# A fused adaLN block of attention and mixture of experts: the experts' rows gated by gathered gate rows before their scatter, and half of the late second rows loaded without accumulation

## The reference

```
mod = (silu(c) @ wmod).reshape(4, 6, 1, 256)
sa, ca, ga, sb, cb, gb = mod rows; ga, gb kept at least 0.25 from zero
h = layernorm(x) * (1 + ca) + sa
x = x + ga * attention(h)               # one head of 128, softmax over 2048 keys
h = layernorm(x) * (1 + cb) + sb
shared = (silu(h @ shared_gate.T) * (h @ shared_up.T)) @ shared_down.T       # I = 512
probs = sigmoid(h @ router_w.T + bias)  # 8 experts
scores, indices = top_k(probs, 2); scores = scores / sum(scores)
combined = sum over the two experts of score * expert(h)                     # I = 512
x = x + gb * (shared + combined)
```

## Time and profile before

| | us |
|---|---|
| median of three runs | 1621.56 |
| the three runs | 1619.24, 1621.56, 1622.91 |
| the profiled execution, its own time | 1623.41 |
| its span on the core | 1621.8 |

### The profile page before, as it was taken

The page is one execution under the profiler, slowest core; times in us unless marked ns, Lnnn a source line. Parts: engine busy times, 40 slices in busy tenths (PEclk is TensorE's granted clock), DMA queues, the critical chain, the costliest instruction groups (busy, mean ns, idle before and its releaser), DMA issues.

```text
span 1621.8 us, 37347 instructions
## 1 busy us (share of the span) xinstructions
PE 1585.6 (98%) x12578; PEld 1525.2 (94%) x12579; DVE 1204.2 (74%) x2492; ACT 994.4 (61%) x1735; POOL 528.8 (33%) x597
## 2 busy tenths in 40 slices
PE   8999999999999999999989999999999999999998
PEld 6799999999999998999989999999999999999987
DVE  6678787777778777898776676766666666666687
ACT  5566666666665556666655666666666666666653
POOL 2545445232300001477761222222222222222321
PEclk9999999999999999999999999999999999999999
DMA  3233343111101326322243132133133231111796
GB/s 124 85 117 125 118 143 124 53 46 45 35 27 37 134 111 186 109 96 92 95 149 95 57 104 65 58 110 110 58 98 94 88 107 62 55 61 41 185 268 184
DMA packets 69610, 160.36 MB, mean 99 GB/s; under 512 B 12932, under 2 KB 17924, under 8 KB 68872
## 3 DMA queue, kind: packets, MB, share of 16 engines
q1 hardware_dynamic: 44872, 93.96, 17.4%
q0 software_dynamic: 23248, 62.97, 13.2%
q10 hardware_dynamic: 1392, 2.10, 0.4%
HBM read 90.75 MB, written 68.24 MB: 98 GB/s over the span
## 4 chain that ended last, share of the span: by engine, by line
PE 48%; DVE 6%; DMA 3%; issue 1%; POOL 1%; ACT 1%; POOLq 0%; DVEq 0%; ACTq 0%; SPq 0%
PE f_bank L957 30%; PE f_bank L32 5%; PE f_bank L34 5%; PE f_bank L33 5%; PE f_bank L939 2%; DMA w_all<-y_rows 2%; POOL x_rows L1420 1%; DVE f_prod L1012 1%; DVE f_aT_lo L1004 1%; DMA y_rows<-more_rows,goes_to 1%; DVE xT_lo L1085 1%; PE f_bank L930 1%; DVE more_rows L1053 0%; DVE more_rows L1059 0%; DVE Z L1763 0%
## 5 line engine op out<-in xcount | busy, mean ns | idle before, releaser
L957 PE MATMUL f_bank<-xT_hi,w_cur_hi 128*128 128x256 f32 x1136 | 322.0, 283 | 0.7 <-ACT f_silu_g L992 0.7
L957 PE MATMUL f_bank<-xT_hi,w_cur_lo 128*128 128x256 f32 x1136 | 321.9, 283 | 0.0
L957 PE MATMUL f_bank<-xT_lo,w_cur_hi 128*128 128x256 f32 x1136 | 321.9, 283 | 0.0
L1438 POOL DMA_INDIRECT y_rows<-more_rows,goes_to x142 | 139.0, 979 | 436.1 <-ACT more_rows L1536 250.2
L1917 DVE TENSOR_TENSOR w_cur_lo<-w_all,w_cur_hi 128x1024 fp32r<-128x1024 f32 x142 | 173.5, 1222 | 63.4 <-ACT w_cur_hi L1503 63.4
L1012 DVE TENSOR_TENSOR f_prod<-f_silu_g,f_bank 128x512 f32<-128x512 f32 x206 | 141.6, 687 | 104.2 <-PE f_bank L957 102.5
L957 PEld LDWEIGHTS f_bank<-xT_hi,w_cur_hi 128*128 128x128 f32 x1136 | 218.0, 192 | 0.8 <-issue 0.8
L957 PEld LDWEIGHTS f_bank<-xT_hi,w_cur_lo 128*128 128x128 f32 x1136 | 218.4, 192 | 0.0
L957 PEld LDWEIGHTS f_bank<-xT_lo,w_cur_hi 128*128 128x128 f32 x1136 | 218.2, 192 | 0.0
L957 PE MATMUL f_bank<-xT_hi,w_shared 128*128 128x256 f32 x1024 | 204.1, 287 | 3.8 <-DVE xT_lo L1744 3.3
L418 ACT ACTIVATE prob<-s_pair,negmax 128x1024 f32<-128x1024 f32 x128 | 142.0, 1114 | 90.4 <-DVE negmax L770 90.4
(11 more groups left out here) (295 smaller groups left out, 4392.7 us busy)
## 6 DMA issues: line engine op xcount, KB each, us to landing
more_rows<-x_rows POOLq DMA_DIRECT2D x71, 260.0 KB, 3.0
XS<-in_x SPq DMA_DIRECT2D x32, 256.0 KB, 3.2
XR<-in_x SPq DMA_DIRECT2D x32, 256.0 KB, 2.9
x<-XR SPq DMA_DIRECT2D x32, 256.0 KB, 2.1
Z<-x SPq DMA_DIRECT2D x4, 2048.0 KB, 11.6
w_all<-y_rows SPq DMA_DIRECT2D x32, 256.0 KB, 5.8
w_all<-y_rows POOLq DMA_DIRECT2D x32, 256.0 KB, 7.0
out<-Z SPq DMA_DIRECT2D x31, 256.0 KB, 4.9
```

The source lines that it names most:

```text
L957: mm = pe.matmul(out[:, 2 * P * i:2 * P * i + 2 * P], w, x, start=(c == 0 and n == 0), stop=(c == HC - 1 and n == 2))
L1438: pool.indirect_dma_start(d.y_rows, bass.IndirectOffsetOnAxis(ap=goes_to[:, par, t:t + 1], axis=0), y[:, t, :], None).then_inc(y_sent[t], 16)
```

## The change

1. **Experts' outputs are gated before they are scattered.** SP writes the four gate rows to a new small DRAM tensor `gates` (4 x 256). For each pair, DVE works out each row's batch from `goes_to` (one more small instruction in `tell`, so `told` counts five per pair), POOL fetches each row's gate with an indirect DMA into `gate_rows` (`fetch_gates`, two per pair), and DVE multiplies the two output tiles at once (`gate_outputs`, 128 x 512, in the next step, ahead of that step's second product). The scatter waits for this multiply (`y_gated`) instead of ACT's copy.
2. **The shared gate goes into the weights.** `shared_down` is now split four times, once for each batch, multiplied by that batch's gate row on POOL: 14 pieces instead of 11. The down weights of the second to fourth batch are loaded when their tiles come near (`load_down`; batches 1 and 3 into a new tile `w_down`, batch 2 over batch 0). `gated` goes; `shared_out` adds PSUM to `Z` directly, early and late; `add_late` and `gate_chunk` go.
3. **Late chunks.** Chunks are taken in order. For slots 0, 2, 4 and 6 of eight (`BESIDE`) SP loads the second row plainly beside the first, and DVE adds both with two instructions; for the others POOL's accumulating DMA stays and DVE adds once. The scattered rows are laid out by batch, so `tokens` and `y_v` change. The last product of DVE moves behind the chunks, ahead of the tail.
4. **The plan of the pairs** is spread over steps 34 to 38 instead of 34 to 37, and the first split of weights comes a step later.
5. **Prologue.** SP loads two chunks of x, then waits for the modulation's columns before the third. ACT waits for wqkv and writes its high part before it issues the loads of the mask, wo and the modulation's rows.
6. ACT writes the first two normalised rows somewhat earlier at the end of the attention, and in the last pair one `single_high` ahead of the outputs.

```diff
-            for m in range(NG + 4):
+            chunk(0)
+            chunk(1)
+            sp.wait_ge(cols_loaded, 16)
+            for m in range(2, NG + 4):
                 chunk(m)
...
             def split_piece(i):
-                pool.wait_ge(piece_in, 16 * i + 16)
+                pool.wait_ge(piece_in, loads_up_to(i))
+                if of_gated(i):
+                    by_chunk = piece_raw[:].rearrange("p (c h) -> p c h", h=H)
+                    pool.tensor_tensor(by_chunk, by_chunk, gate_row[:].unsqueeze(1).to_broadcast([P, W // H, H]),
+                                       ALU.mult).then_inc(piece_split, 1)
+                    pool.wait_ge(piece_split, splits_up_to(i) - 2)
                 pool.tensor_copy(piece_hi[:], piece_raw[:]).then_inc(piece_split, 1)
-                pool.wait_ge(piece_split, 2 * i + 1)
+                pool.wait_ge(piece_split, splits_up_to(i) - 1)
                 pool.tensor_tensor(piece_raw[:].bitcast(F32R), piece_raw[:], piece_hi[:].bitcast(F32),
                                    ALU.subtract).then_inc(piece_split, 1)
...
             act.dma_start(w_raw, wqkv).then_inc(w_loaded, 16)
             act.wait_ge(c_loaded, 16)
             act.activation(ce[:], cT[:], ACT.Exp, scale=-1.0).then_inc(silu_c, 1)
+            act.wait_ge(w_loaded, 16)
+            act.activation(w_hi[:], w_raw, ACT.Copy).then_inc(w_split, 1)
+            act.dma_start(wo_raw, wo).then_inc(wo_loaded, 16)
+            act.dma_start(mask_i[:], mask).then_inc(wo_loaded, 16)
             for n in range(2):
                 o = 2 * H + 512 * n
                 act.dma_start(wmod_rows[:, n], wm[:, :, o:o + 512]).then_inc(rows_loaded, 16)
-            act.dma_start(wo_raw, wo).then_inc(wo_loaded, 16)
-            act.dma_start(mask_i[:], mask).then_inc(wo_loaded, 16)
-            act.wait_ge(w_loaded, 16)
-            act.activation(w_hi[:], w_raw, ACT.Copy).then_inc(w_split, 1)
...
-            sp.wait_ge(gy_done, ALL)
-            sp.wait_ge(sent[0], ONCE * (GROUPS // RING))
+            sp.wait_ge(f.y_out, ALL)
+            for i in range(2):
+                sp.wait_ge(sent[i], ONCE * (GROUPS // RING))
             sp.wait_ge(d.w_ready, 64)
...
             def load(k):
-                n = C * chunk_order[k]
-                sp.dma_start(slots[:, k % SLOTS], y_v[0, :, n:n + C, :]).then_inc(y_in[k % SLOTS], 16)
-
+                n = C * k
+                sp.dma_start(slots[:, k % SLOTS], y_v[0, n // TB, :, n % TB:n % TB + C, :]).then_inc(y_in[k % SLOTS], 16)
+                if k % SLOTS in BESIDE:
+                    sp.dma_start(second[:, k % SLOTS], y_v[1, n // TB, :, n % TB:n % TB + C, :]
+                                 ).then_inc(y_sum[k % SLOTS], 16)
...
-            def scatter(j, par):
-                for t in range(2):
-                    if t == 1 or inside(j - 1, NP):
-                        hold(pool, d, y_sent[1 - t], 16 * j + 16 * t)
-                    hold(pool, d, y_copied, 2 * j + t + 1)
-                    pool.indirect_dma_start(d.y_rows, bass.IndirectOffsetOnAxis(ap=goes_to[:, par, t:t + 1], axis=0),
-                                            y[:, t, :], None).then_inc(y_sent[t], 16)
+            def scatter(j, par, t):
+                if t == 1 or inside(j - 1, NP):
+                    hold(pool, d, y_sent[1 - t], 16 * j + 16 * t)
+                hold(pool, d, y_gated, j + 1)
+                pool.indirect_dma_start(d.y_rows, bass.IndirectOffsetOnAxis(ap=goes_to[:, par, t:t + 1], axis=0),
+                                        y[:, t, :], None).then_inc(y_sent[t], 16)
+
+            def fetch_gates(j, par, t):
+                hold(pool, d, told, 5 * j + 5)
+                if inside(j - 1, NP):
+                    hold(pool, d, y_gated, j)
+                pool.indirect_dma_start(gate_rows[:, t, :], None, d.gates,
+                                        bass.IndirectOffsetOnAxis(ap=batch[:, par, t:t + 1], axis=0)
+                                        ).then_inc(gate_in[t], 16)
...
+                for t in range(2):
+                    if inside(j - 1, NP):
+                        scatter(j - 1, 1 - par, t)
+                    fetch_gates(j, par, t)
...
-            def gated(m):
+            chunks_added = []
+
+            def shared_out(m):
                 dve.wait_ge(f.y_mm, m + 1)
-                if m == 0:
-                    dve.wait_ge(gate_loaded, 80)
-                dve.tensor_tensor(gys[m >= L0][:, m % 2, :], f.y_bank[m % 2][:, 0:H], rows[:, tile_of(m) // TB, 0:H],
-                                  ALU.mult).then_inc(f.y_out, 1)
-
-            def shared_out(m):
-                dve.wait_ge(f.y_out, shared_count(m))
+                k = tile_of(m) // C
+                if k in chunks_added:
+                    dve.wait_ge(out_done, k + 1)
                 z = Z[:, d.home(tile_of(m)), :]
-                dve.tensor_tensor(z, gys[m >= L0][:, m % 2, :], z, ALU.add).then_inc(gy_done, 1)
+                dve.tensor_tensor(z, f.y_bank[m % 2][:, 0:H], z, ALU.add).then_inc(f.y_out, 1)
```

On DVE, in the pair step and in the late stage:

```diff
                 dve.tensor_tensor(score[:, par, :], score[:, par, :], ride[:, par, :, 2], ALU.add).then_inc(told, 1)
+                dve.tensor_scalar(batch[:, par, :], goes_to[:, par, :], (P * TB).bit_length() - 1, NB - 1,
+                                  ALU.logical_shift_right, ALU.bitwise_and).then_inc(told, 1)
+
+            def gate_outputs(j):
+                dve.wait_ge(y_copied, 2 * j + 2)
+                for t in range(2):
+                    hold(dve, d, gate_in[t], 16 * j + 16)
+                dve.tensor_tensor(y, y, gate_rows, ALU.mult).then_inc(y_gated, 1)
...
+            def output_chunk(k, tiles_added):
+                n = C * k
+                own = Z[:, d.home(n):d.home(n) + C, :]
+                dve.wait_ge(f.y_out, min(tiles_added, n + C))
                 dve.wait_ge(y_sum[k % SLOTS], 16 * (k // SLOTS + 1))
-                c = chunk_order[k]
-                if ALL + FIRST <= C * c < NT - C:
-                    dve.wait_ge(f.y_out, shared_count(L0 + C * c + C - 1 - ALL))
-                gate = rows[:, C * c // TB, 0:H].unsqueeze(1).to_broadcast([P, C, H])
-                dve.tensor_tensor(slots[:, k % SLOTS], slots[:, k % SLOTS], gate, ALU.mult).then_inc(gated_done, 1)
-
-            def output_chunk(k):
-                n = C * chunk_order[k]
-                own = Z[:, d.home(n):d.home(n) + C, :]
-                dve.wait_ge(gy_done, min(ALL + FIRST, max(ALL, n + C)))
-                dve.wait_ge(gated_done, k + 1)
+                if k % SLOTS in BESIDE:
+                    dve.wait_ge(y_in[k % SLOTS], 16 * (k // SLOTS + 1))
+                    dve.tensor_tensor(own, own, second[:, k % SLOTS], ALU.add).then_inc(second_added, 1)
+                    dve.wait_ge(second_added, len([c for c in range(k + 1) if c % SLOTS in BESIDE]))
                 dve.tensor_tensor(own, own, slots[:, k % SLOTS], ALU.add).then_inc(out_done, 1)
...
@@ -1978,11 +2041,12 @@
                     plan_counts()
                 if n == STEPS + 3:
                     plan_ends()
+                if n == STEPS + 4:
                     plan_starts()
-                if n == STEPS + 4:
                     plan_behind()
+                if n == STEPS + 5:
                     plan_experts()
-                if n == STEPS + 5:
+                if n == STEPS + 6:
                     plan_moves()
                     plan_rows()
...
+                else:
+                    gate_outputs(j - 1)
                 f.dve_products(dve, m1, f.up_home(k1))
 
             pairs(dve, step)
             for i in range(LATE):
                 m = L0 + i
-                if 3 <= i < 3 + FIRST:
-                    gated(m - 3)
+                if i == 2:
+                    gate_outputs(NP - 1)
+                if i >= 3:
...
-                f.dve_products(dve, m, f.up_home(m))
+                if i < LATE - 1:
+                    f.dve_products(dve, m, f.up_home(m))
                 for k in chunks_of[i]:
-                    gate_chunk(k)
-                    output_chunk(k)
+                    output_chunk(k, ALL + max(0, i - 2))
```

170 lines of the change are left out of this document (96 added, 74 removed).

## The result

The changed kernel took 1668.82 us in the median of three runs (1667.47 to 1672.28) where the kernel before took 1621.56: a ratio of 1.0293, 95% interval 1.0278 to 1.0308. It is slower by 47 us. The prediction was 1620, with a range up to 1636.

What follows compares the result with a forecast made beforehand. PE was taken to bound the kernel nearly everywhere. Terms -0.7 - 2.8 - 0.35 + 1.7 + 9 - 4.4 - 3.7 = -1.25 took the profiled 1623.4 us to 1622.2, the median 1621.56 to 1620; range 1612 to 1636.

Steps and rivals of the forecast that it cites:

- the landing g: Experts' stage: time for gather 1 to land, put at 2.4 to 3.0 us and taken as 2.75.
- What bounds the kernel, prologue: PE sets the time nearly everywhere, only its 36 us idle can be won; delaying the third x chunk gives -0.7 us.
- The ring: Experts' stage: multiply, scatter 0, scatter 1, gather 1, next multiply; 6.23 + g, taken as 8.98 us, within the 9.06 period.
- rival 1: Experts' stage: the ring sets the period once g is over 2.83; 1630 us at g = 2.9, 1637 at 3.0; chance 0.28.
- What doesn't fit is a transfer that lands late.: Experts' stage: late scatters reach PE with 6 us, gather 1 adds half as much; loss +9 us, bounds +3 and +16.
- DVE itself: Experts' stage: multiply, small instruction and waits delay the pair's second product, yet PE gets `aT_lo` with 0.2 us to spare.
- rival 3: Experts' stage: DVE's waits ahead of the multiply take 0.3 us more, `aT_lo` 0.1 late per pair; 1632 us; chance 0.08.
- ScalarE's second copy: Experts' stage: it waits for scatter 1 to land, 1099.3 instead of 1098.34, its silu some 0.2 us late; no cost.
- Early stage: Before the pairs: `xT_lo` waits vanish, -2.8 us; placing moves up by `gated`, -0.35; slowed clock behind PE's wait, +1.7.
- Late stage and tail: After the pairs: less DVE work per chunk, -4.4 us; tail gap shrinks to 1.9 and last multiply goes, -3.7 us.
- The rule of the Trainium skill: Experts' stage: gather into SBUF would land no later than a scatter, ring 8.6 us; the forecast set it aside.

Runs made afterwards that it cites:

- the controls: The kernel before and the changed kernel, both run unchanged on one chip: 1621.03 us and 1670.09 us (1.0298).
- the table of 512 rows: Changed kernel with each batch's gate row stored 128 times, so no two reads of a gather share a row: 1765.01 us, 1.0247 to the kernel before.
- two buffers: Changed kernel with both gathers ahead of scatter 1, DVE's multiply ahead of `is_first`, and output rows in two buffers: 1619.85 us, 0.9993 to the kernel before.
- the halves: Kernel with two buffers, DVE's multiply split per output tile, the first in DVE's wait for the weights' high part: 1612.80 us, 0.9945 to the kernel before.
- all of it together: Kernel with two buffers plus the multiply in halves, first eight late chunks plain, and gate table of 512 rows: 1607.46 us, 0.9914 to the kernel before.

## Why the prediction was wrong, point by point

The forecast was 1620 us and 1668.8 came. Three steps failed, in order of size: the price of late transfers (some 38 us in the pairs where 9 was taken), DVE's queue and the landing g, which both put a calm pair at 9.3 us (18 us), and the late stage with the tail (7.6 us). The early stage gave 4.3 us more than said, which hid a part of that.

- **What bounds the kernel, prologue.** PE set the time before, as said; in the changed kernel it did not in the pairs. The prologue gave 0.8 us between the two traces, 0.7 was said, but that is luck. The modulation's load took 6.2 us in that one trace of the kernel before, and 5.0 and 4.8 us in its two other traces; the changed kernel's three have 4.8 to 4.9. On the chip of the controls PE's first product that waits for it began at 6.53 us before and 6.50 after.
- **The ring: mechanism right, choice of its terms wrong.** Four of its five terms were within 0.04 us: 1.52 (said 1.52), 3.34 (3.35), 1.28 (1.26), and DVE's reaction 0.14 (0.1). The failed term is the gather's landing, "I take g = 2.75", bounds 2.4 to 3.0; it was 3.1. The upper bound came from halving the difference between loads and stores with the bytes. No row of before had a gather or a read of one address by all, so the bound was no bound. With 3.1 the rule of rival 1 gives a ring of 9.33, which is the calm pair's 9.3, so rival 1 was the case, with the chance of 0.28. But a right g would not have saved the forecast: with the table of 512 rows it was 2.8, and the median pair was 9.32 all the same.
- **"What doesn't fit is a transfer that lands late."** Wrong in size. For the case of rival 1 the prediction priced lateness at 14 us. The pairs lost 56.0 us; the calm ring of 9.32 against 9.07 is 18 of them, so lateness cost 38. The working took it from the 45 waits of rows 10, for scatter 0 in the place in which it then stood, and gave the gather half as much. The gather had more (mean landing 3.3 us, median 3.1). Scatter 0 also stood elsewhere: 8.6 us after PE turned the pair's rows, and 3.6 us before the change; whether that put it in the way of more loads is not shown. At g = 3.1 the rule of rival 1 gives 19 + 14 = 33 us for the pairs, and 56 came.
- **DVE itself**, "0.2 to spare". This failed in the changed kernel already. The prediction moved the product by the multiply and the small instruction, 0.6 us, and held only `aT_lo` against PE. It put nothing for the multiply's waits, which take 0.19 or 0.28 us of DVE even when they are met (only rival 3 had them, as 0.3 us), and it didn't see that the chain closes: product, `aT_lo`, down product, ScalarE's copy and high part of the weights, DVE's split, multiply. That ring took 9.3 us. It cost nothing extra beside the gather's ring of the same length, so the number hid it; it is why the table of 512 rows won so little. So rival 3, with its chance of 0.08, was at work beside rival 1: 0.23 us per pair in the changed kernel's order, and 0.06 with two buffers, where 0.1 was said.
- **ScalarE's second copy**, "no cost". Wrong: PE waited ten times for silu, 7.9 us, and 1.3% of the time went with the copy's wait alone (from 1.0131 to 0.9993). The multiply in the chain of the weights' split was another 0.5% (to 0.9945).
- **Early stage.** The waits vanished as said, and PE's wait ahead of the first pair was 2.35 us, without a slow clock (in another trace of the changed kernel it was 2.63 us, with one). What failed is "moves up only by the `gated` that stood ahead of the placing, 0.35 us". The last group's scatters started at 795.6 instead of 800.5 us, so the chain moved by 4.9 us and not by 0.35. That DVE's backlog had set them, and not the last instruction ahead, is argued and not shown. The stage gave 5.7 us where 1.45 was said, and 5.8 us between the two controls on one chip.

```profile
800.46 0.96 POOL L1420 DMA_INDIRECT x_rows<-more_rows,place_i  x1 [1.25 <-DVE place_i L1828]
795.62 0.96 POOL L1466 DMA_INDIRECT x_rows<-more_rows,place_i  x1 [0.76 <-DVE place_i L1896]
843.42 0.66 PE L963 MATMUL f_bank<-ident,more_rows 128*128 128x128 f32 x4 [2.35 <-DMA more_rows<-x_rows]
```

- **Late stage and tail.** Said -8.1, came -0.5. The term that failed is the 3 us: DVE's wait for the first odd chunk was to grow from 1.5 to about 3 us; it grew to 7.71. Counted from PE's cut at 1544.7 (before 1495.3), the last scatter landed after 25 us instead of 19, where 1.9 us later was said; the slot's own load, now the third of twelve, landed 5.1 us behind it instead of 2.9; and the accumulation took 8.3 us from there, little more than the 7.8 before. The tail's gap fell to 1.84 us as said, and that was said to leave the clock alone for 1.3 of the 1.7 us; the clock was halved behind it all the same. The plain loads do pay when the first chunks are plain too: -5.6 us.
- **The rule of the Trainium skill** that a write to HBM has the longer fixed part than one to SBUF (DMA: Bandwidth & Descriptors, "Anatomy of one DMA — SWDGE (gpsimd) path") didn't carry over to the gather: 3.1 us into SBUF against 2.4 for the scatter to HBM. The measurement decides. 0.3 of the 0.7 us went when each read had its own row; where the rest lies is not shown.

## What to carry to other kernels

When a change puts a transfer between two steps of a loop, add up every cycle of waits that it closes, over each engine's queue and each buffer that is used again, and hold each against the period. Follow each until it closes: a chain that is held against one waiting engine only looks roomy. A cycle near the period is over it for part of the time, and then late landings count nearly in full: the one over ScalarE's second copy was put at 8.6 us against 9.07 and still cost 1.3%. Cutting the longest cycle only shows the next, and two can be equally long: here four were cut one after the other (gather behind scatter 1, `is_first`, the single output buffer, the multiply in the weights' split), and only the last cut made the change pay. A bound that comes from transfers of another kind is no bound: g was held under 3.0 by plain loads and stores, came at 3.1, and the answer turned at 2.83.

## What the runs showed of the hardware

- An indirect gather of 128 rows of 1 KB into SBUF landed in 3.1 us when all read four rows of DRAM and in 2.8 us when each read its own; a scatter of the same size to DRAM landed in 2.4 us (medians).
- Chips differ by stage, not by a factor: the same program took 1621 us on two and 1713 to 1721 us on three, nearly all of it in one stage (85 us in the trace, with a granted clock of 0.87 there), while its loop ran at 9.07 us on both kinds. A loop with little slack in a cycle of waits ran at 9.13 us on one kind and at 10.6 us on the other.
- The length of a PE gap alone didn't tell whether the clock was halved behind it. In the trace of the changed kernel it was behind 1.84 us in the tail, and not behind 2.35 us ahead of the first pair nor behind 3.07 us inside the pairs (at 1085.55). The tail's gap of 1.84 or 1.85 us was followed by half the clock in that kernel's three traces and not in those of the halves and of all of it together.
